# Flamingo block (gated cross-attention and top-2 experts): the low part of the turned context made by TensorE and ScalarE instead of VectorE, with other slots

## What is computed

```python
def attention(x, context):                     # x: layernorm of the rows
    q, k, v = x @ Wq, context @ Wk, context @ Wv      # split into 16 heads of 16
    attn = softmax(einsum('bhid,bhjd->bhij', q, k) * 16 ** -0.5)
    return einsum('bhij,bhjd->bhid', attn, v) @ Wo    # heads joined again
x = x + tanh(g_xattn) * attention(layernorm(x), ctx_768)
x = x + tanh(g_ffn) * experts(layernorm(x))    # per row the two best of 8 experts,
                                               # down(silu(gate) * up), weighted by their probabilities
```

## Time and profile before

| | us |
|---|---|
| median of 3 runs | 561.27 (557.2 to 562.57) |
| profiled execution | 561.69 |
| its span, first to last instruction | 559.9 |

### The profile page before, as it was taken

How to read it: one execution, slowest core, us unless ns; L and a number is a source line. 1 busy time by engine, 2 the same in 40 slices (tenths; PEclk the granted TensorE clock), 3 DMA queues, 4 the chain that set the end, 5 groups by cost and what they waited for, 6 DMA issues and landing times. The chain is left out here.

```text
span 559.9 us, 15117 instructions
## 1 busy us (share of the span) xinstructions
PE 475.1 (85%) x4723; PEld 433.4 (77%) x4724; DVE 407.3 (73%) x871; ACT 324.5 (58%) x625; POOL 297.7 (53%) x268
## 2 busy tenths in 40 slices
PE   2986999999999999999988524899899999999920
PEld 1875889998889988989877523698799999999820
DVE  5965889998999989999996486687865545555410
ACT  4642556676676567667555595677855455455510
POOL 5093466665557656655686206144657765654440
PEclk9988999999999999999997555899999999999975
DMA  8566677775567466555403296576734433433333
GB/s 210 148 164 149 158 186 179 185 185 125 136 160 188 108 174 182 131 155 113 99 13 109 70 355 213 186 232 198 142 51 75 73 51 66 66 52 51 39 39 131
DMA packets 69022, 74.88 MB, mean 134 GB/s; under 512 B 28744, under 2 KB 57248, under 8 KB 68784
## 3 DMA queue, kind: packets, MB, share of 16 engines
q1 hardware_dynamic: 60912, 63.23, 42.3%
q0 software_dynamic: 8064, 11.06, 12.1%
HBM read 42.51 MB, written 14.98 MB: 103 GB/s over the span
## 5 line engine op out<-in xcount | busy, mean ns | idle before, releaser
L366 POOL TENSOR_TENSOR PL<-PT 125x448 f16<-125x448 f32 x112 | 109.6, 986 | 104.9 <-ACT PT L499 104.8
L499 ACT ACTIVATE PT<-bank 125x448 f32<-125x448 f32 x192 | 100.9, 543 | 86.1 <-PE bank L630 85.8
L787 DVE TENSOR_REDUCE mx<-bank 112x1 f32<-112x375 f32 x256 | 125.0, 538 | 20.6 <-PE bank L612 19.4
L1242 POOL DMA_INDIRECT acc_scr<-ys,slot_row x42 | 67.0, 1595 | 81.7 <-ACT ys L1316 72.7
L630 PE MATMUL bank<-QS,KS 98*125 98x256 f32 x384 | 82.7, 305 | 4.4 <-DMA QS<-nm 3.4
L612 PE MATMUL bank<-KS,QS 97*112 97x376 f32 x256 | 80.3, 354 | 3.1 <-DMA KS<-bias_scr 1.6
L1569 DVE SCALAR_TENSOR_TENSOR hf<-bank,ub,sg 128x256 f32<-128x256 f32 x84 | 38.4, 482 | 49.7 <-ACT sg L1293 49.6
L1384 PE MATMUL bank<-xH,GH 128*128 128x256 f16 x336 | 65.7, 278 | 6.2 <-DVE xL L1548 3.6
L630 PEld LDWEIGHTS bank<-QS,KS 98*125 98x125 f32 x384 | 63.7, 193 | 6.2 <-DMA QS<-nm 2.9
L1384 PE MATMUL bank<-xL,GH 128*128 128x256 f16 x336 | 65.3, 277 | 0.3 <-issue 0.3
L1384 PE MATMUL bank<-xH,GL 128*128 128x256 f16 x336 | 65.1, 276 | 0.0
(11 more groups left out here) (218 smaller groups left out, 1045.4 us busy)
## 6 DMA issues: line engine op xcount, KB each, us to landing
KS<-kH SPq DMA_DIRECT2D x128, 94.0 KB, 2.2
KS<-kL SPq DMA_DIRECT2D x64, 94.0 KB, 2.2
QS<-q_scr SPq DMA_DIRECT2D x96, 56.0 KB
ctx_sb<-in_ctx SPq DMA_DIRECT2D x16, 281.2 KB
wsq<-in_L_ffn_gate_w SPq DMA_DIRECT2D x8, 512.0 KB, 3.7
wsq<-in_L_ffn_up_w SPq DMA_DIRECT2D x8, 512.0 KB, 4.5
w_raw<-in_L_ffn_gate_w SPq DMA_DIRECT2D x8, 512.0 KB
w_raw<-in_L_ffn_up_w SPq DMA_DIRECT2D x8, 512.0 KB
```

Source lines behind the costliest of these rows:

```text
L366: pool.tensor_tensor(PL[:, 2 * k:2 * k + 2, :, 0:N], PT[:, 2 * k:2 * k + 2, :, 0:N], PH[:, 2 * k:2 * k + 2, :, 0:N], ALU.subtract).then_in ...
L499: act.activation(PT[:, 2 * k:2 * k + 2, :, 0:N].rearrange("p a e i -> p (a e) i"), psST[k % 2][0:JP].rearrange("p (a i) -> p a i", i=NI)[: ...
L787: dve.tensor_reduce(mx[:, hd:hd + 1], psS[hd % SBANKS][0:N, 0:M], AX.X, ALU.max).then_inc(v_max, 1)
L1242: pool.indirect_dma_start(acc_scr, bass.IndirectOffsetOnAxis(ap=slot[:, TH * t + k:TH * t + k + 1].bitcast(U32), axis=0), ys[:, u, k, :], ...
```

## The change

`ctx_T` turns the context into misc as before, but each bank is now one accumulation group of three transposing matmuls. Later in the same step, in slot 11, the new `ctx_rest` multiplies cTH by minus the identity and adds it to misc, so that misc holds context minus its high part; in slot 13 ACT copies that into cTL (`transposed_low`). DVE's subtraction goes from the steps; for the first two batches, whose context is turned before or at the start of the pipeline, it stays. `project_k` waits for ACT's copy instead of DVE's subtraction. The identity is negated once by ACT before the first loads are used. The slots are changed too: six lows on POOL and six on DVE instead of seven and five, other slots for the heads, the means, the variances, the squares and POOL's `values`. In the routing chain one semaphore of its own is replaced by the chain's common one.

```diff
+        minus = sb("minus", [CK, CK], F32R)
...
-        POOL = [k for k in (0, 1, 2, 3, 6, 7, 10) if k < SB]
+        POOL = [k for k in (1, 2, 3, 4, 7, 8) if k < SB]
...
-        heads_at = {0: (0,), 1: (1, 2, 3), 2: (4, 5), 4: (6, 7), 5: (8, 9), 6: (10, 11), 7: (12, 13, 14), 8: (15,)}
+        heads_at = {0: (0, 1), 1: (2, 3), 2: (4,), 3: (5,), 4: (6, 7), 5: (8, 9, 10), 6: (11, 12, 13), 7: (14,), 8: (15,)}
...
-        ST, AG, XT, LG, RT = 10, 12, 10, 12, 14
-
-        VR, LV = 2, 10
-        SQ = 7
+        ST, AG, XT, LG, RT = 7, 13, 10, 12, 14
+
+        VR, LV = 3, 10
+        SQ = 5
+        TR, TL = 11, 13
...
+        of_ctx = lambda b: b - 1
...
+        def second(i, c):
+
+            return isinstance(i, int) and NB * i + c < 2
...
+                def transposed_low(i, c):
+                    b, h, u = at(i, c)
+                    act.wait_ge(p_R, of_ctx(b))
+                    act.activation(cTL[:, :, 0:M], misc[0:CK].rearrange("p (c n) -> p c n", c=2)[:, :, 0:M],
+                                   ACT.Copy).then_inc(a_R, 1)
...
+                        if k == TL and live(i, c, -1) and not second(i, c + 1):
+                            transposed_low(i, c + 1)
...
+                act.wait_ge(s_id, 1)
+                act.activation(minus[:], ident[0:CK, 0:CK], ACT.Copy, scale=-1.0)
...
-                            mm = pe.transpose(misc[0:CK, 512 * k + JP * t:512 * k + JP * (t + 1)],
-                                              ctx_sb[:, u, t, CK * k:CK * (k + 1)], ident[0:JP, 0:JP])
+                            mm = pe.matmul(misc[0:CK, 512 * k + JP * t:512 * k + JP * (t + 1)],
+                                           ctx_sb[:, u, t, CK * k:CK * (k + 1)], ident[0:JP, 0:JP],
+                                           start=(t == 0), stop=(t == JT - 1), is_transpose=True)
...
-                    if m == 0:
+                    if m == 0 and second(i, c):
                         pe.wait_ge(v_T, b + 1)
+                    elif m == 0:
+                        pe.wait_ge(a_R, of_ctx(b))
...
+                def ctx_rest(i, c):
+
+                    b, h, u = at(i, c)
+                    pe.wait_ge(a_T, b + 1)
+                    for k in range(2):
+                        mm = pe.matmul(misc[0:CK, 512 * k:512 * k + MP], minus[:], cTH[:, k, :],
+                                       start=False, stop=True, skip_group_check=True)
+                    mm.then_inc(p_R, 1)
...
+                        if s == TR and live(i, c, -1) and not second(i, c + 1):
+                            ctx_rest(i, c + 1)
...
-                        if s == CT + 1 and live(i, c, -1) and not starts(i, c):
-                            transposed(i, c + 1)
...
-                dve.reciprocal(rstd[:], rstd[:]).then_inc(e_rs, 1)
-                dve.wait_ge(e_rs, 1)
+                link(dve.reciprocal(rstd[:], rstd[:]))
```

More of the change, by code:

```diff
@@ L177, in attention @@
         p_ST, p_PV, p_OT, p_Wo = (sem(n) for n in ("pe_scoresT", "pe_pv", "pe_oT", "pe_wo"))
+        p_R, a_R = sem("pe_ctx_rest"), sem("act_ctx_rest")
         a_T, a_K, a_V, a_E, a_O = (sem(n) for n in ("act_ctxT", "act_k", "act_v", "act_exp", "act_oT"))
@@ L1093, in experts @@
             a_col, e_off = isem("act_col"), isem("dve_offset")
-            e_ve, e_rs, e_sh, e_low, e_tw = (isem(n) for n in ("dve_ve2", "dve_rs2", "dve_shift", "dve_low", "dve_tw"))
+            e_ve, e_sh, e_low, e_tw = (isem(n) for n in ("dve_ve2", "dve_shift", "dve_low", "dve_tw"))
             e_ch, e_sc, e_r, e_both, e_ck, e_col, e_slot, e_rw, e_te = (isem(n) for n in (
```

## The result

The changed kernel takes 557.83 us in the median of 20 runs (554.49 to 560.3); the kernel before, on the same chip, 560.31 (20 runs, 557.2 to 562.57). The ratio is 0.995, interval 0.9935 to 0.9965: 2.5 us faster, less than the 1% (5.6 us) that counts here as a difference. The forecast was 2.1 us slower, and within 1%. The time did stay within 1% and inside the range, but it moved the other way. The profiled execution of after is the slowest of its 20, 560.3 us, with a span of 558.6; so whole spans are not compared here, only stretches at full TensorE clock.

A forecast was written before the change was run, and what follows sets the result against it. Each step was taken as a loop of DVE's head and PE's dense tail: -0.09 + 0.35 - 0.16 = +0.10 us, +1.3 over 13 steps, plus 0.8 in the drain, +2.1 in all: 563.5 us, range 557 to 570.5.

The forecast's parts named there:

- The head: Steady step up to `max_T`, DVE's part: idle found but eaten by low 0, end T+11.45 against T+11.54, -0.09 us.
- Rival C: DVE's head: low 0 not absorbed, 0.72 us a step, 9.4 in all plus 0.8, so 571.5 us; chance 0.12.
- PE's wait ahead of `max_T`: End of the head: PE waits about 0.47 us a step for DVE's row maxima; 0.2 to 0.4 expected after.
- rival B: Head: PE only waits less, -0.15 us a step, -2 in all; far end, all waits gone, 557.5 us; chance 0.17.
- The price of the pair: PE's dense tail: two added `ctx_rest` matmuls cost 0.35 us a step, bounds 0.30 to 0.51.
- the term of the tail: From `max_T` to next `scores_T`: +0.35 us for the pair, -0.16 for PE's wait on the last low.
- The sixth low: Drain, second of the last two batches' steps: one more low on DVE, 0.53 to 0.97 us, taken as 0.8.
- rival D: Tail: POOL's last_values falls on DVE's lows, 0.34 us too late a step, 568 us with the drain; chance 0.07.
- ScalarE's copy: ACT's added copy into cTL, 0.80 us at about T+15.5 to 16.3, hidden, 0.7 us before `project_k` needs it.
- Squares, row means and variances: ACT's moved work: squares (1.91 us) ahead of exp 5 covered by 0.4 us, the others only reordered; all at nothing.
- rival E: ACT late with the squares or the new copy: 0.2 to 0.4 us a step, 566 to 569 us; chance 0.06.
- F: Nothing measurable, since loads of the SP queue set steps: 561.5 us; chance 0.58 together with A, the forecast itself.

The follow-up runs named there:

- the exchanges: Low 8 and low 10 swapped between POOL and DVE in the last two batches alone: kernel before with low 10 on DVE 558.28 us; changed kernel with it on POOL 560.56 us.
- a second pair: Changed kernel with a second, equal pair of matmuls by a zero matrix right behind ctx_rest's: 562.33 us, ratio to before 1.0037.
- the move only: Kernel before with its own slots, heads and lows, only cTL made by ctx_rest and ACT's copy: 559.47 us, ratio 0.9991.
- the second measurement: The changed kernel, unchanged, measured again beside the kernel before: 558.05 us, ratio 0.9955.
- the fastest kernel: Changed kernel with low 6 on POOL as well, and all twelve lows of the last batch on DVE: 554.81 us, ratio to before 0.9892.
- the move with low 10 on DVE: Kernel before with cTL made by ctx_rest and ACT, and low 8 on POOL, low 10 on DVE instead of the reverse: 557.82 us, ratio 0.9953.

## Why the prediction was wrong

**Where the 4.6 us lie.** Forecast was +2.1, measured −2.5. 2.1 us of the difference lie in the 13 periods (forecast +1.3, measured −0.8), and 2.5 outside them, which the exchanges put into the drain (forecast +0.8, measured −1.7, of which the profiles place 0.1). Two steps of the prediction failed: the cover of the added pair, and what moving low 10 off POOL does to the drain, which had no term in the sum.

**The head was right.** Forecast was an end of the sixteenth maximum at T+11.45 and a gain of 0.09; measured T+11.44, and 0.11 for the head. That low 0 eats the idle and no more was shown by its removal: the steady steps stayed as they were. Rival C (low 0 not absorbed, 571.5) is refuted by that. One reading beside it was off: PE's wait ahead of `max_T` was put at 0.47 us, and the row says 0.31. With no wait `max_T` starts 0.47 behind the last `scores_T` (194.82 to 195.29 with low 6 on POOL), in before 0.79 behind it, so 0.32. Only rival B's far end rests on it, and would be 559.6, not 557.5.

**The price of the pair was right, its cover was not.** 0.35 us was forecast and is what a second pair costs. The first step that failed is the term of the tail, +0.19 us a step: only the 0.16 us that PE waits for low 11 was set against it. A second wait stood in the same timeline: the next to last `sums` started 0.41 behind the router's matmuls instead of 0.32, 0.09 us of waiting, for low 10 by its place. The prediction did note that this wait goes, and put no number on it. The wait of 0.16 comes from low 10 as well. The prediction took low 11, 0.78 us long, to be met by POOL's product; but it ends at 185.06, 0.48 behind POOL's low 10, and at its usual 0.61 it would have ended at 184.89, ahead of its `sums`. POOL, timeline of before:

```profile
183.64 0.94 POOL L366 TENSOR_TENSOR PL<-PT 125x448 f16<-125x448 f32 x1 [2.97 <-ACT PT L499]
```

The added pair covers both waits. The rest is 0.02: in after the new pair and the first pair of `project_o` take 0.64 together (182.18 to 182.82), where that first pair alone took 0.31 (183.44 to 183.75 in before's timeline), so 0.33 for the new one. 0.33 − 0.16 − 0.09 = +0.08; measured is 4.51 for 4.44, +0.07, where the forecast had 4.63; the move only gave 0 to +0.06. With the head a step is 0.04 us shorter, not 0.10 longer, so −0.5 us in 13 steps for +1.3.

**The drain was half seen.** This is the second step that failed, and the larger one. The sixth low was forecast at 0.8 us, and the last period went from 13.76 to 14.59, +0.83. But what low 10 leaves behind on POOL was read for a danger only (rival D) and not for what it would cure. The prediction's own show the collision in before: two lows of 2.88, the first held by POOL's low 10 and the second by POOL's product of the values, 1.85. It was entered as a place where a further low is dear. With low 10 on DVE, POOL's last_values starts 0.4 us after `max_T` instead of 3.5 us (180.13 − 179.72 against 184.53 − 180.99), beside `normalise`, and the collision is gone: −0.9 us from the last `max_T` on where that is at full clock (5.06 to 4.14), which pays the 0.83 back. Rival D's mechanism is true; its sign was wrong here, for the change ends it rather than making it. The prediction had POOL's product from T+12.2 to T+14.05, on low 9; it ran from T+11.99 to T+13.45 (196.22 and 1.47 us), so that no low met it. What moved to `normalise` (0.84 for 0.29) makes the three lows end at T+15.51 (198.06 + 1.68 − 184.23) instead of T+15.1, and DVE idle before its second `normalise` for 0.3 us (3.5 in twelve) instead of 0.9. It is hidden in steady steps: no `sums` waits for them. The Trainium skill, "SBUF — State Buffer", SBUF: two separate sides, says that a DVE instruction with two SBUF inputs and a GpSimd one that reads SBUF exclude each other on a shared port pair for a whole instruction. The traces agree, for the low (it ends 0.48 us behind POOL's instruction), and for the small product in `normalise` (0.15 behind it); the maxima (0.53 to 0.55 us with and without POOL) and the key's low part (0.93), which have an input in PSUM, are not stretched.

**What is left of the gain.** In us: twelve steps at 0.04, −0.5; the first of the thirteen periods −0.28 (15.88 to 15.60); last period +0.83; behind it −0.9. That makes −0.85 of −2.5. For the rest there is a trace, though no isolated cause. The mean granted clock is 0.9349 in the runs of after (0.9338 in the second measurement) and 0.928 to 0.931 in four sets of before; within one kernel 0.001 of it goes with some 0.24 us (all sets together; 0.08 to 0.35 in single ones). So 0.003 to 0.004 makes 0.7 to 1.0 us. Most experiments go the same way: 0.9343 and 0.9362 where before's heads and lows have low 10 on DVE in the drain, 0.9306 where after has it taken back, 0.9407 in the fastest kernel. But two with low 10 on DVE don't: 0.9319 with low 0 on POOL, 0.9293 with the old heads. Much of the time at the low clock lies from the drain on: before 301.1 to 348.9 us, its second profile 292.8 to 296.2, 299.7 to 309.9 and 313.3 to 350.9, after 292.6 to 309.6 and 313.0 to 350.6, the second profile of after 298.9 to 302.3 and 309.1 to 346.7, the move with low 10 on DVE 310.2 to 344.3 only. So they differ within one kernel as much as between the two: from the last `max_T` to the end of the last routed copy after takes 26.91 us at a granted clock of 0.59 in one profile and 22.33 at 0.80 in the other, before 26.51 and 26.43 at 0.67 and 0.65. That fewer such stretches follow where PE idles less in the drain was not tried by itself, with an idle of set length put there, and stays open, and with it about 1.6 of the 2.5 us: their place (the drain) is shown by the two exchanges, their mechanism is not. The exchange in before alone has the same gap: 2.7 us gained, 0.8 of them placed. The prediction named a shorter stretch at the low clock only as a gain that rival B could have on top, and its own sum had no term for the clock.

**The other steps.** ScalarE's copy is hidden: it runs 183.34 to 184.14, and `project_k` wants it at about 185.13 in the next step. Squares, row means and variances cost nothing that a wait shows: rival E (566 to 569) did not come. Rival B's number, 557.5, is nearly the time measured, by luck and not by its mechanism: PE's wait ahead of `max_T` did not go (3.5 us in twelve before, 4.2 after). F, nothing at all, is outside the interval. The routing edit: last routed copy to the table of experts 19.6 us before and after, so nothing.

## What to carry to other kernels

Price the fill and the drain of a pipelined loop apart from its steady step: a wait that is covered 13 times may be bare in the fourteenth, and here an exchange in two batches of 16 moved as much as the whole change. When an instruction leaves an engine, follow what moves up behind it, for what it cures as well as for what it may hit. And before adding work to a dense stretch, list every wait in it, down to 0.1 us: they are what it is paid from, and the next addition is paid in full (0 to 0.07 us a step for the first pair, 0.35 for the second).

## What the runs showed of the hardware

- DVE's instructions with two SBUF inputs and POOL's products and lows take turns, and the ends show it. In the 16 profiles, from 100 us on, 220 lows of DVE that came while POOL was at work end 0.48 us behind POOL's instruction (0.477 to 0.485), and 125 small products of `normalise` end 0.15 behind it (0.144 to 0.150). The other way round, 76 products of the values on POOL end 1.33 behind a low of DVE, and 115 of POOL's lows 0.79 behind one. So the low takes 0.61 us by itself and up to 1.86, the small product 0.29 and up to 1.17 (with low 6 on POOL), POOL's product 1.47 and 1.85, POOL's low 0.93 and up to 1.85, by where they meet.
- DVE's instructions with an input in PSUM are not held: in before, from 100 to 290 us, 165 maxima beside POOL's instructions take 0.53 to 0.55 us, 24 others the same.
- The granted clock of one and the same kernel varies from run to run (0.923 to 0.941 in 12 runs of after with the drain's exchange taken back, whose times went from 563.1 to 558.5 us), and 0.001 of it goes with some 0.24 us of 560. That is more than the steady steps of this change are worth.
- A matmul pair of 96x376 in fp32r with a 96*96 weight costs 0.34 to 0.35 us start to start, like one with 128 rows of output (0.34 to 0.35 in `project_k`).
